# A gated graph layer on one core: the edge bias by ScalarE, the message in the sums' bank, and a re-ordered head

## The reference

```
m[e]   = relu([h[src], h[dst]] @ W1[t] + b1[t]) @ W2[t] + b2[t]
agg    = segment_sum(m, dst)
gi, gh = agg @ W_ih.T + b_ih,  h @ W_hh.T + b_hh
r, z   = sigmoid(i_r + h_r), sigmoid(i_z + h_z)
n      = tanh(i_n + r * h_n)
out    = x + (1 - z) * n + z * h
```

## Time and profile before

| | |
|---|---|
| median of 3 runs | 1737.02 us (1736.04 to 1738.2) |
| the profiled execution's own time | 1735.05 us |
| its span | 1733.2 us |
| PE busy | 1616.9 us (93%) |
| PE weight loads busy | 1421.4 us (82%) |
| DVE busy | 1629.0 us (94%) |
| ACT busy | 1458.7 us (84%) |
| POOL busy | 1003.4 us (58%) |

### The profile page before, as it was taken

The page is one execution under the profiler, slowest core; times in us unless marked ns, Lnnn a source line. Parts: engine busy times, 40 slices in busy tenths (PEclk is TensorE's granted clock), DMA queues, the critical chain, the costliest instruction groups (busy, mean ns, idle before and its releaser), DMA issues. The chain is left out here.

```text
span 1733.2 us, 43005 instructions
## 1 busy us (share of the span) xinstructions
PE 1616.9 (93%) x10182; PEld 1421.4 (82%) x10182; DVE 1629.0 (94%) x4752; ACT 1458.7 (84%) x3404; POOL 1003.4 (58%) x1325
## 2 busy tenths in 40 slices
PE   0337999999999999999999999999999999999998
PEld 0326888888888888888888888888888888888887
DVE  8987999999999999999999999999999999999986
ACT  0126999999999999999999999999999999999896
POOL 5755656666666666655555555565655555555500
PEclk9956999999999999999999999999999999999999
DMA  2235777777777777777777777777777777777653
GB/s 84 70 87 154 193 195 206 203 200 200 203 200 203 199 199 203 198 200 196 199 198 200 200 195 201 196 200 195 197 201 194 201 196 199 197 196 200 188 143 100
DMA packets 477080, 320.07 MB, mean 185 GB/s; under 512 B 105917, under 2 KB 463117, under 8 KB 476974
## 3 DMA queue, kind: packets, MB, share of 16 engines
q10 hardware_dynamic: 261792, 156.12, 29.3%
q1 hardware_dynamic: 186638, 107.42, 25.5%
q0 software_dynamic: 28544, 55.41, 13.1%
HBM read 212.08 MB, written 107.07 MB: 184 GB/s over the span
## 5 line engine op out<-in xcount | busy, mean ns | idle before, releaser
L613 POOL DMA_INDIRECT e_x<-in_x,rows_now x816 | 824.4, 1010 | 248.4 <-issue 239.0
L1258 ACT ACTIVATE e_h<-e_x,shift,rstd 128x128 f32<-128x128 f32 x816 | 355.8, 486 | 90.0 <-DVE shift L1114 57.0
L1275 ACT ACTIVATE n_h<-n_x,shift,rstd 128x128 f32<-128x128 f32 x784 | 385.3, 492 | 2.9 <-issue 2.9
L1414 PE MATMUL bank<-n_h_hi,whh_hi 128*128 128x512 f32 x588 | 249.2, 424 | 1.2 <-ACT n_zc L1366 1.2
L1414 PE MATMUL bank<-n_a_hi,wih_hi 128*128 128x512 f32 x588 | 246.4, 419 | 0.9 <-DVE bank L1154 0.9
L1494 PE MATMUL bank<-n_sel,n_win 128*128 128x256 f32 x1568 | 234.7, 292 | 0.4 <-DVE n_sel L1142 0.4
L1416 PE MATMUL bank<-n_a_hi,wih_lo 128*128 128x512 f32 x588 | 232.5, 395 | 0.0
L1416 PE MATMUL bank<-n_h_hi,whh_lo 128*128 128x512 f32 x588 | 231.7, 394 | 0.0
L1415 PE MATMUL bank<-n_h_lo,whh_hi 128*128 128x512 f32 x588 | 231.2, 393 | 0.0
L1142 DVE TENSOR_SCALAR n_sel<-iota,n_rel 128x256 fp32r<-128x256 f32 x784 | 229.6, 357 | 0.1
L1415 PE MATMUL bank<-n_a_lo,wih_hi 128*128 128x512 f32 x588 | 229.6, 391 | 0.0
(11 more groups left out here) (193 smaller groups left out, 3812.4 us busy)
## 6 DMA issues: line engine op xcount, KB each, us to landing
n_win<-messages SPq DMA_DIRECT2D x1568, 64.2 KB
messages<-e_msg ACTq DMA_DIRECT2D x204, 257.0 KB, 2.9
n_x<-in_x ACTq DMA_DIRECT2D x195, 256.0 KB
out<-n_out ACTq DMA_DIRECT2D x195, 256.0 KB
e_x<-in_x,rows_now POOLq DMA_INDIRECT x816
rows_now<-lists SPq DMA_DIRECT2D x204, 2.0 KB
lists<-picks,list_rows POOLq DMA_INDIRECT x54, 2.8
w<-in_W SPq DMA_DIRECT2D x1, 512.0 KB, 5.0
```

Source lines behind the costliest of these rows:

```text
L613: G.indirect_dma_start(e_x[:, s, 2 * end + t, :], None, x, bass.IndirectOffsetOnAxis(ap=rows_now[:, s, t, end:end + 1], axis=0)).then_inc( ...
L1258: last = A.activation(e_h[:, s % 2, k, :], e_x[:, s, k, :], ACT.Relu, scale=rstd[:, slot, col + k:col + k + 1], bias=shift[:, slot, col + ...
L1275: last = A.activation(n_h[:, s % 2, cols], n_x[:, s, cols], ACT.Relu, scale=rstd[:, slot, col + 4 + k:col + 5 + k], bias=shift[:, slot, co ...
L1414: T.matmul(o, w_hi, v_hi, start=start, stop=False, skip_group_check=onto)
```

## The change

1. **The bias.** PE's product for b2 (L1518) goes. ACT copies two rows of b2, which lie in SBUF on all partitions (`b2_two`, now a buffer of its own), into PSUM (`seed_message`, an ACTIVATE with Copy, 128x256), and PE's two W2 products add onto it. PE waits for it (`e_seeded`). It stands behind n_n and the load of n_x, ahead of n_zc.
2. **The bank.** The message lies in the right half of bank 2 (BA), which the group's sums fill whole. So the seed waits for `n_alo` (the sums have been split) and `e_low` (the last unit's low half is done), and the sums wait for `e_low`. The hidden layer, in bank 7, no longer waits for `e_low`.
3. **The head.** DVE forms the low half first in a step of the head; ACT starts the load of n_x at the step's start and the store of the message behind e_ht. The check is cut in two: `check_inputs` in step 14, `check_bounds` in step 15 with PE's sum, the flag (`flag_general`) in step 16.
4. **Newton.** A round has three operations in place of four (nine in place of twelve for each four steps), by two VectorE instructions that do two operations each.
5. **The windows.** SP waits for stores in even steps alone: for unit g + 4 ahead of the four windows of types 0 and 1, for unit g + 5 ahead of those of types 2 and 3, and the windows are started in that order.

The diff, cut to its core:

```
@@ sync, step
+                    for pair_ in range(2):
+                        if m % 2 == 0:
+                            q = g + AHEAD - 1 + pair_
+                            if not isinstance(g, int):
+                                qs = (m - LAG + 2 + AHEAD - 1 + pair_) % UNROLL
+                                sp.wait_ge(e_stored[qs], uses(q, qs, UNROLL, 16))
+                            else:
+                                for stored in range(pair_ if g == 0 else q, min(q + 1, UNITS), 2):
+                                    sp.wait_ge(e_stored[stored % UNROLL], uses(stored, stored % UNROLL, UNROLL, 16))
+                        for half in range(2):
+                            for t in (2 * pair_, 2 * pair_ + 1):
...
@@ vector, newton
-                dve.wait_ge(ln_ops, first * (LN_ROOTS // 4) + n + 1)
+                dve.wait_ge(ln_ops, first * (LN_ROOTS // 4) + 4 + n)
...
-                elif n % 4 == 1:
-                    ins = V.tensor_tensor(root_u[:], root_t[:], half_var[:], ALU.mult)
-                elif n % 4 == 2:
-                    ins = V.tensor_scalar(root_t[:], root_u[:], -1.0, 1.5, ALU.mult, ALU.add)
+                elif n % 3 == 1:
+                    ins = V.scalar_tensor_tensor(out=root_u[:], in0=root_t[:], scalar=-1.0, in1=half_var[:],
+                                                 op0=ALU.mult, op1=ALU.mult)
...
+                    ins = V.scalar_tensor_tensor(out=new, in0=root_u[:], scalar=1.5, in1=old[:], op0=ALU.add, op1=ALU.mult)
...
@@ vector, step
-                in_head = isinstance(i, int) and i < LAG - 2
-                if not in_head:
-                    low_half(i, m)
+                low_half(i, m)
+                if isinstance(i, int) and i == GENERAL_STEP:
+                    flag_general()
...
-                if in_head:
-                    low_half(i, m)
...
+                if isinstance(i, int) and i == CHECK_STEP + 1:
+                    check_bounds()
@@ scalar
+            def seed_message(i, m):
+                q = i - 9
+                if not within(q, UNITS):
+                    return
+                if isinstance(q, int) and q == 0:
+                    act.wait_ge(s_written, 1)
+                if due(q):
+                    act.wait_ge(e_low, q)
+                if within(i - LAG + 1, NG):
+                    act.wait_ge(n_alo, i - LAG + 2)
+                first = 2 * ((m - 9) % 2)
+                A.activation(bank[BA][:, message_part], b2_two[:, first * D:(first + 2) * D], ACT.Copy).then_inc(e_seeded, 1)
...
@@ scalar, step
+                in_head = isinstance(i, int) and i < LAG - 2
+                if in_head:
+                    load_x(i, m)
                 normalise_edges(i, m, (0, 1))
...
-                store_messages(i, m)
+                if not in_head:
+                    store_messages(i, m)
...
+                if in_head:
+                    store_messages(i, m)
                 q, s = i - 9, (m - 9) % 2
...
-                load_x(i, m)
+                if not in_head:
+                    load_x(i, m)
+                seed_message(i, m)
...
-                    A.activation(e_msg[:, s, :, 0:D], bank[BE1][:, message_part].rearrange("p (t d) -> p t d", t=2),
+                    A.activation(e_msg[:, s, :, 0:D], bank[BA][:, message_part].rearrange("p (t d) -> p t d", t=2),
@@ tensor, step
                     if due(g):
                         pe.wait_ge(n_alo, g)
+                    if within(i - 10, UNITS):
+                        pe.wait_ge(e_low, i - 9)
...
                     pe.wait_ge(e_evaced, q + 1)
-                    if due(q):
-                        pe.wait_ge(e_low, q)
...
                     pe.wait_ge(e_relued, q + 1)
                     first = 2 * ((m - 9) % 2)
-                    T.matmul(bank[BE1][:, message_part], ones_r[:], b2_rows[:, first * D:(first + 2) * D],
-                             start=True, stop=False)
+                    pe.wait_ge(e_seeded, q + 1)
                     for t in range(2):
-                        o = bank[BE1][:, 2 * P + t * D:2 * P + (t + 1) * D]
-                        last = T.matmul(o, e_r[:, s, t * P:(t + 1) * P], w2[:, first + t, :], start=False, stop=t == 1)
+                        o = bank[BA][:, 2 * P + t * D:2 * P + (t + 1) * D]
+                        last = T.matmul(o, e_r[:, s, t * P:(t + 1) * P], w2[:, first + t, :], start=False, stop=t == 1,
+                                        skip_group_check=True)
```

More of the change, by code:

```diff
@@ L235, in gnn_layer @@
         descends = borrow(n_zc[:], 0, ECOLS)
-        b2_two, b2_hi, b2_lo, b2_parts = (
-            e_msg[:].rearrange("p r t w -> p (r t w)")[:, at * TYPES * D:(at + 1) * TYPES * D] for at in range(4))
-        b2_two, b2_parts = b2_two.bitcast(F32), b2_parts.bitcast(F32)
+        b2_hi, b2_lo, b2_parts = (
+            e_msg[:].rearrange("p r t w -> p (r t w)")[:, at * TYPES * D:(at + 1) * TYPES * D] for at in range(3))
+        b2_parts = b2_parts.bitcast(F32)
         ends = n_d[:].rearrange("p r w -> p (r w)").bitcast(I32).rearrange("p (k e c) -> p k e c", k=SEGMENTS, e=2)
@@ L390, in gnn_layer @@
         e_high = sem("e_high")
+        e_seeded = sem("e_seeded")
+        s_written = sem("s_written")
         e_low = sem("e_low")
@@ L550, in step @@
                         "check_inputs flags any start past its list's last window, and general_sums replaces them all")[1]
-                    if isinstance(g, int):
-                        for q in range(0 if g == 0 else min(g + AHEAD, UNITS), min(g + AHEAD + 1, UNITS)):
-                            sp.wait_ge(e_stored[q % UNROLL], uses(q, q % UNROLL, UNROLL, 16))
-                    else:
-                        q, qs = g + AHEAD, (m - LAG + 2 + AHEAD) % UNROLL
-                        sp.wait_ge(e_stored[qs], uses(q, qs, UNROLL, 16))
@@ L557, in step @@
                     if isinstance(g, int) and due(g - 3):
                         sp.wait_ge(n_summed, g - 3)
-                    for half in range(2):
-                        for t in range(TYPES):
-                            at = t % 2 * WIN
-                            if half == 1 and t == 3 and within(g + LAG - 6, UNITS):
-                                sp.wait_ge(e_tagged, g + LAG - 6)
-                            sp.dma_start(n_win[at:at + WIN, s, 2 * half + t // 2, 0:ROW].bitcast(F32),
-                                         messages[bass.ds(firsts[4 * half + t], WIN), 0:ROW]
-                                         ).then_inc(n_windowed[s], 16)
+                    for pair_ in range(2):
[9 more added lines that the diff above has]
+                            for t in (2 * pair_, 2 * pair_ + 1):
+                                at = t % 2 * WIN
+                                if half == 1 and t == 3 and within(g + LAG - 6, UNITS):
+                                    sp.wait_ge(e_tagged, g + LAG - 6)
+                                sp.dma_start(n_win[at:at + WIN, s, 2 * half + t // 2, 0:ROW].bitcast(F32),
+                                             messages[bass.ds(firsts[4 * half + t], WIN), 0:ROW]
+                                             ).then_inc(n_windowed[s], 16)
@@ L1012, in general_sums @@
                         dve.wait_ge(g_messaged, 4 * c + 1)
[L1013 removed]
+                        V.tensor_scalar(g_msg, bank[BIN][:, 0:D], g_types[:, 0:1], None, ALU.mult).then_inc(g_messaged, 1)
                         for t in range(1, TYPES):
                             dve.wait_ge(g_messaged, 4 * c + 1 + t)
[L1016 removed]
+                            ins = V.scalar_tensor_tensor(out=g_msg, in0=bank[BIN][:, t * D:(t + 1) * D],
                                                          scalar=g_types[:, t:t + 1], in1=g_msg,
@@ L1104, in ln_part @@
                     V.tensor_scalar(root[:].bitcast(I32), half_var[:].bitcast(I32), -0.5, float(RSQRT_SEED - (1 << 22)),
-                                    ALU.mult, ALU.add).then_inc(ln_ops, 1)
+                                    ALU.mult, ALU.add).then_inc(ln_ops, 4)
                 elif third == 1:
                     newton(first, place, slot)
-                elif third == 2 and place < 3:
-                    newton(first, 8 + place, slot)
-                    if place == 2:
-                        newton(first, 11, slot)
+                elif (third, place) == (2, 0):
+                    newton(first, 8, slot)
                 elif (third, place) == (2, 3):
@@ L1410, in _ @@
             T.matmul(bank[BIN][:], ones_r[:], b2_rows[:], start=True, stop=True)
+            pe.wait_ge(s_rowed, SEGMENTS)
+            T.matmul(bank[BA][:], ones_r[:], b2_rows[:], start=True, stop=True).then_inc(s_written, 1)
             def product(o, w_hi, w_lo, v_hi, v_lo, start, stop, onto):
@@ L1447, in general_sums @@
                         pe.wait_ge(g_relued, c + 1)
-                        T.matmul(bank[2][:], ones_r[:], b2_rows[:], start=True, stop=False)
```

(5 more changed lines are left out.)

27 lines of the change are left out of this document (14 added, 13 removed).

## The result

| | us, median | runs | ratio to before, 95% interval |
|---|---|---|---|
| before | 1737.61 | 1736.04 to 1739.39 | |
| after | 1762.93 | 1762.28 to 1763.56 | 1.0145 [1.0129, 1.0161] |

The account below looks back on a forecast made before the run. PE was taken to bound the kernel, always busy, with ACT close behind. To the profiled 1735.05 us came +25 for the ring and -3.5 for the head: 1757, or 1759 as a median, range 1727 to 1775.

Parts of the forecast that it names:

- The ring: Steady steps: message waits for seed, seed for n_n, n_r for gate r, gate r for message; 8.10 us against 7.97, +25 us.
- the 1759: Whole kernel: forecast median, from 1757 for the profiled execution, taken to lie 2 us under the median.
- The seed's length: ACT's copy of 256 columns into PSUM, in every step: said to take 0.39 us, ends 0.35 and 0.45.
- The rival built on the faster port: Copy into PSUM plus hand-over take 0.3 us or less: ring 7.89, kernel faster, median 1722; chance 0.20.
- What b2's product costs PE: PE's product L1518, 0.12 us a step: removing it saves only about 0.06, at most 12 us, since gate r waits for n_zc.
- the fast rival: The seed comes early enough for PE's message: 0.06 us a step and 3.5 of the head saved, median 1722; chance 0.20.
- n_zc keeps its place: ACT in each step: the seed's 0.30 us fits, just, into the 0.34 us idle before n_zc, so n_zc isn't delayed.
- The rival of a cover too short: ACT before n_zc: seed takes over 0.4 us or starts late, delaying n_zc; step 8.24, 1787 us; chance 0.10.
- The bank, Newton, the windows in the steady part at nothing: Steady steps: moving the message's bank, shorter Newton rounds on DVE and reordered windows each claimed to change nothing.
- The head: Before the first gate r: earlier load, Newton rounds and flag start the windows 3.7 us earlier; -3.5 us net, ends -6 and 0.
- DVE's new wait: Head: DVE waits for the next unit's copy before its statistics, 1.1 us, in place of the removed 4.22 us wait.
- What would show it: Signs in the profile: PE under 100%, 0.1 to 0.2 us idle before the message's weights, changed ACT waits, step of 8.10.

Follow-up runs that it names:

- e4: Changed kernel without b2 in the messages; ACT makes the same copy at its place, into SBUF, and nobody waits for it: 1731.43 us, ratio 0.9973.
- e5: Changed kernel, but PE waits before the message for the seed alone and not also for e_relued: 1751.12 us, ratio 1.0090.
- e8: Changed kernel with a seed of 128 columns in place of 256, leaving out the bias of each unit's second type: 1744.27 us, ratio 1.0047.
- e3: Changed kernel with b2 left out altogether, no seed, the message still in the changed kernel's bank: 1728.73 us, ratio 0.9956.
- e2: Changed kernel with b2 as a product on PE again, in the old bank; new head, Newton rounds and window order kept: 1731.21 us, ratio 0.9968.
- e9: e2 with gate r's product waiting for n_zc alone, its two other waits put ahead of the product before: 1723.72 us, ratio 0.9924.
- e12: e2 with the four-operation Newton rounds of the kernel before: 1731.65 us, ratio 0.9968.
- e7: Changed kernel with the copy ahead of n_n, n_xh behind n_a_lo on DVE, and single waits at message and gate r: 1739.37 us, ratio 1.0025.

## Why the prediction was right, point by point

- **The ring** of n_r, n_n, seed, message and gate r is shown: the wait in every step, e4 (same copy into SBUF, no wait: 31.5 us faster, 30 by the ratios), e5 and e8 (hand-over and length one for one). Its parts, said and measured in the mean of all steps but the first: n_r to n_n 4.44 and 4.48; 0.57 and 0.57; the seed 0.39 and 0.40; seed to product 0.12 and 0.15; message to gate r 0.91 and 0.88; 1.67 and 1.68. Sum 8.10 and 8.15. The middle one of the steps grew by 0.130, as forecast. The mean grew by 0.157: +30.7 us where +25 stood. The largest miss is the first part, read from one step and stretched by the longer ones (before, too, its mean is 4.49); the hand-over is next. Against them stands that the step of before was put at 7.97, from a count in 800 us, where the openings in the earlier trace rows give 1560.53 / 195 = 8.00. For the profiled execution 1757 had been said and 1762.28 came; the 1759 looks nearer to the median of 1762.93 because that lies 0.6 above the profiled one and not 2.
- **The seed's length.** 0.403 us, within its bounds of 0.35 and 0.45. The same copy into SBUF, in e4, took 0.431. So the Trainium skill's sentence that PSUM is ScalarE's faster destination ("ScalarE: Activation LUTs", Step-by-step: what each stage is for) is borne out here by 0.03 us. The rival built on the faster port needed the two parts to take 0.3 together; they took 0.55.
- **What b2's product costs PE.** This term was mis-sized: "say 0.06: at most 12 us". e3 against e2 shows 0.004 a step. The error is the hand-over to gate r, 0.12 and not 0.05 to 0.10, taken from a place with one semaphore. The earlier trace rows had the right size already, from n_zc's end at 809.07 to gate r at 809.21; I put that down to PE's order, as if b2 had held gate r up, and wrote that PE never waits for ACT. It did, in the kernel before: from the second step on gate r opened 0.14 after n_zc's end 177 times of 194, and 0.05 after it the other times. A busy share of 100% didn't show it, since products overlap: from the message to gate r it was 0.91 us there, and 0.82 in e9, where the hand-over is short. It didn't touch the forecast, which took the ring as it stood, but the fast rival's 1722 rested on it: by e3 even a free bias gives 1729.
- **n_zc keeps its place**: right, it starts 0.03 after z's last product ends at 808.94. The rival of a cover too short didn't come.
- **The bank, Newton, the windows in the steady part at nothing**: e12 shows it for Newton, and e2's step of 7.995 against 8.003 for Newton and the windows together. e2 has the old bank; for the new one there is e3, which shares it and has a step of 7.991.
- **The head**, -3.5: measured -3.42, which is luck: the errors cancelled. The flag came at 139.62 and not 140.5, the windows at 142.00 and not 142.8. DVE's new wait was 1.57, not 1.1, though the granted clock was 1.00 there and not half. Between the sums and gate r 0.99 was lost and not 0.2: 0.53 to the seed, for which the message waits once more, and 0.47 to the lower clock, when that rises being luck. The Newton rounds gave 0.61 at the flag where 0.5 had been said, in two traces with unequal clocks. The first step, whose first 3.4 us ran at the low clock, lost another 0.95; in e5, which had the full clock there, it took 8.89 us, so about a third of that is not the clock's.
- **What would show it** came, by and large: PE under 100%, ACT's wait in front of n_r 0.55 (0.5 had been said), that in front of n_zc 0.04 (0.05). The idle time in front of the message's weights is there, but as 0.55 and put down to "issue", where 0.1 to 0.2 and the seed had been said; what PE itself idles is 0.16 a step.

## What to carry to other kernels

A bias product that costs the busiest engine 0.12 us isn't necessarily 0.12 us of time: see which wait opens the next operation, and whether it would open any earlier. Work given to another engine has to be followed round: if what it must come after is itself released by the engine that will wait for it, its length and both hand-overs go into every step, however idle that engine is on average. Moving it ahead in its own queue opens that ring, but delays the rest of the queue, and the next limit may lie within 1% of the first (8.115 after 8.160 here); a list of rings with their lengths, made beforehand, tells how much an escape is worth.

## What was not expected of the hardware

- The hand-over from ScalarE to a TensorE that waits, up to the start of the weight load, took 0.04 to 0.05 us where the instruction had one semaphore to wait for (message in e5, gate r in e7 and e9), and 0.11 to 0.12 where it had two or three (message in the changed kernel, gate r in e2 and e3), though the others had long been met. Leaving the others out, or putting them ahead of the transposes before, gave 11.8 us (e5; 9 by the ratios, 12.7 by the steps) and 7.5 us (e9) with the same work. The Trainium skill ("Perfetto Trace Analysis", Identifying Dependency Chains) says that an instruction which waits for more than one engine may get separate wait instructions ahead of it. That would fit, but the profile lists no such instruction here, so that this is the cause isn't shown. It isn't the number of semaphores alone: in the first step of each turn of the loop (17 of the 194 steps, in before, e2 and e3) gate r opens 0.05 after n_zc although it has the same three waits, and in the kernel before the middle one of these steps takes 7.91 where that of the others takes 7.99. One of them in the kernel before:

```profile
848.30 0.69 ACT L1366 ACTIVATE n_zc<-bank,bneg 128x512 f32<-128x512 f32 x1 [0.27 <-PE bank L1416]
...
849.05 0.50 PE L1414 MATMUL bank<-n_h_hi,whh_hi 128*128 128x512 f32 x1
```

- An ACTIVATE copy of 256 columns: PSUM to SBUF 0.37, SBUF to PSUM 0.403, SBUF to SBUF 0.431 (e4). Of 128 columns, SBUF to PSUM, 0.298: 0.105 less for half.
